# The layers' gathers of a graph network pass over the rows of empty slots

## The reference

```python
ew = edge_attr @ edge_w + edge_b
inv_cnt = [1.0 / maximum(segment_sum(m, dst), 1.0) for m in rel_masks]
for l in range(3):
    residual = x
    msg = relu(x[src] * ew)
    out = zeros((n, 256))
    for i in range(3):
        h = segment_sum(msg * rel_masks[i][:, None], dst) * inv_cnt[i][:, None]
        out = out + h @ weights[l, i]
    out = out + x @ roots[l] + biases[l]
    x = residual + relu(out)
```

## Time and profile before

| | before |
|---|---|
| median of three runs | 7233.64 us |
| span of the profiled execution | 7241.5 us |
| POOL busy | 4792.5 us (66%) |
| PE busy | 4531.8 us (63%) |
| DVE busy | 4522.6 us (62%) |
| ACT busy | 2263.1 us (31%) |
| gathers of the layers, line 564 | 2568, mean 1024 ns |
| moved by DMA | 1152.25 MB, mean 159 GB/s |

### The profile page before, as it was taken

One profiled execution on the slowest core, in us unless ns is written; L12 is line 12 of the kernel. 1 busy time (PEld: TensorE's weight loads), 2 busy tenths in 40 slices (PEclk: granted clock), 3 DMA queues, 4 the chain that ended last, 5 costly groups with the idle time before them and its releaser, 6 DMA issues.

```text
span 7241.5 us, 91193 instructions
## 1 busy us (share of the span) xinstructions
PE 4531.8 (63%) x18049; PEld 2696.2 (37%) x18049; DVE 4522.6 (62%) x10666; ACT 2263.1 (31%) x5474; POOL 4792.5 (66%) x4436
## 2 busy tenths in 40 slices
PE   6499222222788869056676776666666766566588
PEld 2255111111444436034444454333334533333365
DVE  7887555555666677156666645666665566666553
ACT  0088100000566642044444432222222222222231
POOL 0483777776777788777777735777774477777500
PEclk9899555555999989578888878777777877877689
DMA  4100677777566541266666655767666477767700
GB/s 118 19 1 5 216 224 229 228 228 207 145 152 152 152 122 29 54 196 212 209 213 210 211 101 160 212 210 211 209 210 127 135 210 211 211 210 210 171 15 18
DMA packets 515195, 1152.25 MB, mean 159 GB/s; under 512 B 123407, under 2 KB 252530, under 8 KB 514849
## 3 DMA queue, kind: packets, MB, share of 16 engines
q0 software_dynamic: 195328, 458.59, 25.8%
q1 hardware_dynamic: 272516, 553.06, 23.1%
q10 hardware_dynamic: 47136, 138.12, 6.8%
HBM read 865.64 MB, written 282.20 MB: 159 GB/s over the span
## 4 chain that ended last, share of the span: by engine, by line
POOL 47%; issue 25%; PE 14%; DMA 10%; DVE 3%; POOLq 1%; DVEq 0%; ACT 0%; SPq 0%; ACTq 0%
POOL sort_mem L564 27%; POOL recB_d L538 14%; POOL acc_mem L523 6%; PE banks L961 5%; DMA sort_mem<-x_d,x_mem 4%; PE banks L1168 4%; DMA acc_mem<-h_d,z_mem 3%; DMA pay_d<-acc_mem 2%; PE banks L1063 1%; PE banks L1073 1%; PE banks L881 1%; PE banks L1158 1%; DVE xnt_mem L1372 0%; DVE acc_mem L1302 0%; PE banks L937 0%
## 5 line engine op out<-in xcount | busy, mean ns | idle before, releaser
L564 POOL DMA_INDIRECT sort_mem<-x_d,x_mem x2568 | 2629.3, 1024 | 841.3 <-issue 801.6
L1131 PE MATMUL banks<-z_mem 128*128 128x257 f32 x5136 | 2054.7, 542 | 1206.8 <-DVE acc_mem L1536 1082.6
L1131 PEld LDWEIGHTS banks<-z_mem 128*128 128x128 f32 x5136 | 1164.7, 256 | 2083.8 <-DVE acc_mem L1536 1479.5
L1536 DVE TENSOR_TENSOR acc_mem<-acc_mem,banks 128x257 f32 x3376 | 1420.7, 421 | 528.9 <-PE banks L1131 162.0
L803 ACT ACTIVATE z_mem<-z_mem 128x512 f32<-128x512 f32 x1284 | 790.4, 631 | 2387.3 <-DVE z_mem L1718 2387.2
L1718 DVE TENSOR_TENSOR z_mem<-x_mem,sort_mem 128x512 f32<-128x512 f32 x1284 | 833.6, 691 | 961.6 <-DMA sort_mem<-x_d,x_mem 957.3
L538 POOL DMA_INDIRECT recB_d<-sort_mem x800 | 1016.3, 1270 | 267.4 <-issue 244.1
L523 POOL DMA_INDIRECT acc_mem<-h_d,z_mem x808 | 811.3, 1004 | 353.6 <-issue 336.6
L978 PE MATMUL banks<-ident,z_mem 128*128 128x128 f32 x808 | 225.1, 434 | 725.5 <-DVE z_mem L1475 725.5
L1029 PE MATMUL banks<-acc_mem,z_mem 128*128 128x257 f32 x1616 | 545.6, 420 | 142.2 <-DVE acc_mem L1536 126.7
L507 POOL DMA_INDIRECT recA_d<-acc_mem x240 | 299.3, 1247 | 321.0 <-DVEq L1319 248.2
(11 more groups left out here) (278 smaller groups left out, 4961.3 us busy)
## 6 DMA issues: line engine op xcount, KB each, us to landing
x_mem<-ew_d SPq DMA_DIRECT2D x428, 512.0 KB, 4.2
ew_d<-x_mem SPq DMA_DIRECT2D x214, 512.0 KB, 3.0
pay_d<-acc_mem SPq DMA_DIRECT2D x202, 516.0 KB, 3.8
acc_mem<-pay_d ACTq DMA_DIRECT2D x202, 516.0 KB
x_mem<-recB_d SPq DMA_DIRECT2D x642, 68.0 KB
sort_mem<-x_d,x_mem POOLq DMA_INDIRECT x2568
edge_d<-xnt_mem ACTq DMA_DIRECT2D x40, 332.0 KB
sort_mem<-edge_d SPq DMA_DIRECT2D x40, 332.0 KB
```

What stands on the lines that cost most here:

```text
L564: pool.indirect_dma_start(out=xg[h % XG][:, k, :], out_offset=None, in_=x_d, in_offset=bass.IndirectOffsetOnAxis(ap=reci[h][:, k, W_SRC:W_ ...
L1131: m.matmul(bank[5 + tile % 3][:, :AC], oneh[:, Q % 2, k, :], msg[:, Q % 2, k, :], start=True, stop=True)\
L1536: v.tensor_tensor(a_, a_, bank_[:, :AC], ALU.add).then_inc(flushed, 1)
```

## The change

Records of empty slots get 2 * NP_ = 6400 as their source row, which x_d with NP_ = 3200 rows doesn't have. The four gathers of a quad get a bound of 3199 and the word that a row over it is no error but is passed over. Since the places of such rows in the ring then keep what they held, VectorE zeroes the ring once before layer one.

```diff
             g.memset(fill.rearrange("p (t c) -> p t c", c=RW)[:, :, W_SEG:W_SEG + 1], -1.0).then_inc(S("p_const"), 1)
-            pool.wait_ge(S("p_const"), 12)
+            g.memset(fill.bitcast(INT32).rearrange("p (t c) -> p t c", c=RW)[:, :, W_SRC:W_SRC + 1], 2 * NP_).then_inc(S("p_const"), 1)
+            pool.wait_ge(S("p_const"), 13)
             pool.sem_inc(S("fill_ready"), 1)
...
                             pool.indirect_dma_start(
                                 out=xg[h % XG][:, k, :], out_offset=None, in_=x_d,
-                                in_offset=bass.IndirectOffsetOnAxis(ap=reci[h][:, k, W_SRC:W_SRC + 1], axis=0))\
+                                in_offset=bass.IndirectOffsetOnAxis(ap=reci[h][:, k, W_SRC:W_SRC + 1], axis=0),
+                                bounds_check=NP_ - 1, oob_is_err=False)\
                                 .then_inc(S(f"landed{h % XG}"), 16)
...
             st.did(v.memset(msg[:, :, :, D:AC], 1.0))
             dve.wait_ge(S("acc_zeroed"), 1)
+            st.did(v.memset(sort_mem[:, 0:XG * 4 * D], 0.0))
             for k in range(4):
```

## The result

The changed kernel takes 7272.61 us (median of four runs, 7262.56 to 7278.64); the kernel before, beside it, 7236.93 us. The ratio is 1.0047, with a 95% interval of 1.0032 to 1.0061: about 35 us slower, where 77 us faster were forecast. The profiled execution has a span of 7260.6 us, which belongs to the fastest of its four runs, while that of before, 7241.5 us, lies above the median of its own; so the two traces stand only 19 us apart.

A forecast was written before the change was run, and what follows sets the result against it. GpSimd's issue of gathers was taken to bound the layers, the landing only their ends. 7233.6 - 80.3 (tail) + 3.45 (zeroing) = 7156.8 us, plus 2.57 us per nanosecond of x (taken as 0); range 7080 to 7420 us.

The forecast's parts named there:

- x: Extra ns per layer gather from the bound, taken as 0; each ns adds 2.57 us, break-even at 30 ns.
- What bounds the kernel: GpSimd's issue of gathers paces a layer, 5.32 us per quad; landing bounds only its end, 8.04 us per quad.
- The tail: Quads 203 to 213 ending each layer: passing over empty rows saves 30.0, 24.6 and 25.7 us, together 80.3 us.
- the lag of quad 202: Layer one: time from the end of quad 202's last gather to its multiply, read as 1.44 us.
- The partial tiles: Empty rows at the ends of 75 buckets, 4064 per layer: skipping them is worth nothing, being under the issue.
- The zeroing: VectorE's new memset of 4096 columns, on the path before the first gather: 3.45 us more, once.
- The sequencer: Setting up the bound on GpSimd's sequencer costs nothing; the pause between gathers stays 0.30 us.
- The bound on 2568 gathers: Disputed term, on the layers' gathers: price per gather taken as 0, with up to 240 ns (616 us) considered.
- the first rival: Bound paid per row on every gather: 80 ns each, 7362 us; sign: median 1000 ns or more; chance 0.39.
- The estimate of one cycle per row: Within the gather on GpSimd: one more cycle for each of 128 rows, 107 ns per gather, 7431 us.
- Shorter gathers: Skipped rows shorten gathers in the tail and partial tiles: 96 us more gained, 7061 us; chance 0.12.
- No effect: Passed-over rows go to a substitute address; the tail keeps 8.04 us per quad, total 7237 us; chance 0.07.

The follow-up runs named there:

- e5: Kernel before plus only the bound and passing over on the layers' gathers; empty slots still name row 0, ring not zeroed: 7337.45 us, ratio 1.0142.
- e1: Kernel before, but empty slots name source row 25 times their partition (128 different rows); no bound, no zeroing: 7158.43 us, ratio 0.9892.
- e2_spread_bound: Kernel of e1 plus the bound of 3199 with passing over on the layers' gathers; no row out of bounds: 7267.5 us, ratio 1.0046.
- e8: Kernel of e1 with the ring zeroed, each layer gather bringing only rows of partitions 0 to 31, no bound: 7000.43 us, one run.
- e6_four_rows: Kernel before, but empty slots name rows 0, 800, 1600 and 2400, one per 32 partitions; no bound: 7151.29 us, one run.

## Why the prediction was wrong

The step that failed is the price of the bound on each gather, which the sum put at nothing (x = 0); the runs show 52 ns in the median and 38 to 43 on the path. The parts in turn:

**What bounds the kernel: right.** GpSimd's issue sets the pace of a layer and the landing only its end. e5 shows it from one side (dearer issue: slower everywhere but at the end), e1 from the other (other rows: faster at the end only, with the 812 gathers ahead of it at 1.33 us each in both).

**The tail: right, and near in size.** Forecast 80.3 us; e1_spread, which has this term alone, gave 74.3 us (the interval of its ratio is 66 to 90 us). One reading behind the sum was off by one: 4188.70 is the second gather of quad 203, and 4187.13 the first. So 1080.16 us hold 813 gathers, 1.329 us each, and the lag of quad 202 is 3.0 us and not 1.44. The two slips cancel, and 4248.3 stays.

**The partial tiles: right, nothing that shows.** They lie under the issue: ahead of quad 203 a gather of layer one takes 1.36 us from start to start in the changed kernel and in e2_spread_bound, which skips none.

**The zeroing: right in place, 0.9 us too small.** It is where it was said to be, and takes 3.47 us for 3.45. But VectorE also wakes 0.9 us later than before (3079.32 + 16.37 = 3095.69, then 3096.61). All five kernels with this memset show 0.92 us there and all seven without it 0.03, so it belongs to the memset; why, isn't known. From the end of line 548 to the first gather it makes 21.7 us for 17.4, 4.3 more.

```profile
3079.32 16.37 POOL L548 MEMSET acc_mem<- 128x19532 f32 x1 [1.79 <-DMA recB_d<-sort_mem]
...
3096.61 3.47 DVE L1685 MEMSET sort_mem<- 128x4096 f32 x1 [125.30 <-POOL acc_mem L548]
```

**The sequencer: right.** A register move of 29 ns has come in 2568 times, and the pause is 0.30 us as before.

**The bound on 2568 gathers: this step failed.** The text took x = 0, on the ground that the gather's own row is nearer than a form with another direction, and that nothing in that row says that a compare isn't already made. But that row speaks of a gather without the bound, and not at all of the price of one: an absence of evidence was taken for a zero. Measured, x is 52 ns in the median. On the path it is less: the mean gather went from 1024 to 1062 ns, 38 ns, and from e1_spread to e2_spread_bound it is 42.5 ns by the times. With 40 ns the formula on record gives 7156.8 + 103 = 7260 us, and 3 more for the runs of before that it was then measured beside; 7272.6 was measured. Of the other 9 us, 6 are the tail, by e1_spread, and 1 is the zeroing; the rest is small beside the 16 us over which the runs of the changed kernel spread. The point at which the gain is lost, x = 30 ns, was worked out rightly, and the value lies just beyond it. The time lies within the range but on the other side, where the first rival stood. That rival was right in its place and its sign; 80 ns on the path was twice too much, and its reason, a price per row, is not borne out. Its sign in the profile, a median of 1000 ns or more, was missed by a single nanosecond, while no sign of the other rivals appeared.

Why 38 and not 52: sort the gathers by what VectorE was at when each started, that is, by the last instruction that had started and not ended (10 gathers under other instructions are left out).

| VectorE at the start of the gather | before: gathers, mean ns | after: gathers, mean ns |
|---|---|---|
| idle | 950, 946 | 930, 998 |
| flush (one input in PSUM) | 541, 946 | 688, 998 |
| multiply (both inputs in SBUF) | 615, 1106 | 574, 1186 |
| one-hot (both inputs in SBUF) | 452, 1173 | 366, 1151 |

An undisturbed gather costs the whole 52 ns more. But the gathers that start in a multiply or a one-hot became fewer, 940 for 1067, and those in a one-hot are lengthened by 153 ns and not by 227. Spread over all gathers the lengthening falls from 78 to 64 ns, which is the 14 that are missing. e1_spread and e2_spread_bound show the same step (1085 and 955 such gathers). That the slower rhythm does this is argued from the counts, not tested. The Trainium skill, page "SBUF — State Buffer", section "Who interferes with whom", says that a two-input VectorE operation with both inputs in SBUF contends with GpSimd's reads. The trace agrees: the multiply and the one-hot lengthen the gathers, and the flush doesn't.

**The estimate of one cycle per row.** The Trainium skill's "DMA: Bandwidth & Descriptors", section "SWDGE vs HWDGE vs iDMA", has software compute the descriptors. From that I estimated one cycle more per row at 107 ns; the page itself gives no price for a bound. The runs show 43, 37 and 52 ns for 32, 64 and 128 rows: it isn't priced per row.

**Shorter gathers** (the second rival): false. The changed kernel takes 1.00 us for a gather with none of its 128 rows in bounds. Its premise, that a skipped row needs no descriptor, isn't borne out either, since the number of packets has stayed and each skipped row leaves 4 bytes. Even a gather that never names three quarters of the rows (e8) saves only 72 ns.

**No effect** (the third rival): false, since bytes and DMA share fell and the multiplies at the end stand 5.4 us apart. What a skipped row leaves behind, 4 bytes in a packet of 11 ns, costs no time that could be seen here.

**What I would do otherwise.** The gain was 80 us in 129 of 2568 instructions, and the price was on all 2568, with no slack. With a break-even of 30 ns, 3% of a gather, and rows that allowed anything up to 240, I should have given slower the larger chance, and not 0.36.

## What to carry to other kernels

An option that is set on every instruction of a chain that bounds is paid for every time; put its break-even beside the instruction's duration (here 30 of 947 ns) before the gain, and if no row prices it, don't take zero. Padding that names one and the same row is a trap by itself: let empty slots name different valid rows, and the end of the layer runs like its middle at no cost (e1_spread with 128 rows, 1.1% faster than before; e6_four_rows with four, one run, looks the same). And before work is left out, look at what the engine on the path is paid for: here it is the instruction, nearly whatever its number of rows.

## What the runs showed of the hardware

- An indirect gather's time on GpSimd is mostly fixed: 875, 910 and 947 ns for 32, 64 and 128 rows of 1 KB.
- A bound on it costs 43, 37 and 52 ns for 32, 64 and 128 rows (for 128, 52 ns with and without rows out of bounds); as an error and not as a passing over, 65 ns (128 rows).
- A row passed over moves 4 bytes and not 1024 (429.32 MB and not 458.59), leaves the number of packets at 195328, and doesn't shorten the gather.
- 128 reads of one and the same kilobyte per gather hold the DMA engines at a share of 1.00 with 122 GB/s; four different rows are enough to bring it to 0.61 with 201 GB/s. A packet of four rows takes 829 ns in the mean at the first and 204 at the second, while equal packets of another queue stay at 160 beside the first.
- A gather that starts while VectorE runs an operation with both inputs in SBUF takes 1106 ns (multiply) or 1173 ns (one-hot) in the mean; beside an idle VectorE, or a flush with one input in PSUM, 946 ns.
- A VectorE memset as the first instruction behind a long wait started 0.92 us after the wait's end, in five kernels; another instruction in its place started after 0.03 us, in seven.
